# A transformer layer on one core: experts three deep, the routing weight applied as a root ahead of the square, all attention products on VectorE

## What is computed

```python
h = take(tok_weight, x)                                  # (8, 1024, 256)
h = h + attn(layernorm(h))                               # 16 heads of 16; softmax over the 8 positions
z = layernorm(h)
scores = sigmoid(z @ Wg.T)                               # 16 experts in 4 groups
# the best 2 groups, then the best 4 experts; w = 2.5 * score / sum of the four scores
out = sum_e w_e * (relu(z @ W1_e)**2 @ W2_e.T)           # cw[t, e] is 0 for an expert not chosen
h = h + out + relu(z @ Ws1.T)**2 @ Ws2.T                 # the shared expert, two slices wide here
```

## Time and profile before

| | |
|---|---|
| median of 3 runs | 1469.57 us (1466.58 to 1469.63) |
| the profiled execution | 1464.6 us |
| TensorE, matmuls busy | 1267.7 us, 87% |
| VectorE busy | 1189.9 us, 81% |
| ScalarE busy | 679.8 us, 46% |
| GpSimd busy | 689.5 us, 47% |
| mean granted TensorE clock | 0.961 |

### The profile page before, as it was taken

How to read it: one execution, slowest core, us unless ns; L and a number is a source line. 1 busy time by engine, 2 the same in 40 slices (tenths; PEclk the granted TensorE clock), 3 DMA queues, 4 the chain that set the end, 5 groups by cost and what they waited for, 6 DMA issues and landing times.

```text
span 1464.6 us, 22940 instructions
## 1 busy us (share of the span) xinstructions
PE 1267.7 (87%) x7488; PEld 1033.1 (71%) x7488; DVE 1189.9 (81%) x1792; ACT 679.8 (46%) x1138; POOL 689.5 (47%) x753
## 2 busy tenths in 40 slices
PE   4458898889888899888989889898988989989898
PEld 2146767768677687767778677776867768677787
DVE  3868889697987969789797888969798797978854
ACT  2234444544444454444544444454553445445355
POOL 7744535365263635535464363536526363442600
PEclk9579999999999999999999999999999999999999
DMA  2302111111211112111111212112121111212122
GB/s 66 125 16 74 58 60 58 61 62 55 73 62 57 58 44 88 58 61 58 66 65 44 78 67 62 58 46 73 58 73 58 61 58 44 88 44 73 59 73 73
DMA packets 33748, 92.21 MB, mean 63 GB/s; under 512 B 4800, under 2 KB 13376, under 8 KB 33600
## 3 DMA queue, kind: packets, MB, share of 16 engines
q1 hardware_dynamic: 30528, 81.99, 16.7%
q0 software_dynamic: 3072, 8.39, 2.0%
HBM read 81.46 MB, written 8.91 MB: 62 GB/s over the span
## 4 chain that ended last, share of the span: by engine, by line
DVE 39%; PE 31%; issue 19%; POOL 5%; ACT 5%; DMA 1%; DVEq 1%; ACTq 0%; POOLq 0%; SPq 0%
PE psY L900 9%; PE psH L887 8%; DVE ring L684 7%; PE psB L927 5%; DVE p_sb L641 5%; DVE hid_lo L647 5%; PE psA L966 3%; DVE g_gt L723 2%; DVE ring L300 2%; PE psA L978 2%; DVE ring L302 2%; DVE ring L279 1%; DVE k_sb L666 1%; ACT hid_hi L510 1%; DVE stats L659 1%
## 5 line engine op out<-in xcount | busy, mean ns | idle before, releaser
L900 PE MATMUL psY<-w_hi,hid_hi 128*128 128x256 f32 x1152 | 339.0, 294 | 53.6 <-DVE hid_lo L647 50.3
L510 ACT CAST hid_hi<-p_sb 128x512 fp32r<-128x512 f32 x256 | 159.2, 622 | 388.8 <-DVE p_sb L641 379.5
L900 PE MATMUL psY<-w_lo,hid_hi 128*128 128x256 f32 x1152 | 330.5, 287 | 0.0
L900 PE MATMUL psY<-w_hi,hid_lo 128*128 128x256 f32 x1152 | 330.2, 287 | 0.0
L279 POOL TENSOR_TENSOR ring<-q_sb,k_sb 128x1024 f32<-128x1024 f32 x64 | 169.1, 2653 | 309.1 <-PE psA L940 205.2
L900 PEld LDWEIGHTS psY<-w_hi,hid_hi 128*128 128x128 f32 x1152 | 223.6, 194 | 107.4 <-DVE hid_lo L647 72.6
L647 DVE TENSOR_TENSOR hid_lo<-p_sb,hid_hi 128x512 fp32r<-128x512 f32 x256 | 214.6, 838 | 93.4 <-ACT hid_hi L510 73.7
L887 PE MATMUL psH<-xT_hi,w_hi 128*128 128x512 f32 x576 | 235.6, 409 | 10.9 <-issue 8.7
L641 DVE TENSOR_TENSOR p_sb<-r_sb,cwB 128x512 f32<-128x512 f32 x256 | 214.2, 837 | 34.1 <-ACT r_sb L499 27.2
L900 PEld LDWEIGHTS psY<-w_lo,hid_hi 128*128 128x128 f32 x1152 | 224.6, 195 | 9.8
L887 PE MATMUL psH<-xT_lo,w_hi 128*128 128x512 f32 x576 | 230.2, 400 | 0.0
(11 more groups left out here) (133 smaller groups left out, 2137.5 us busy)
## 6 DMA issues: line engine op xcount, KB each, us to landing
cwB<-cw_dram SPq DMA_DIRECT2D x128, 512.0 KB, 3.7
out<-h SPq DMA_DIRECT2D x32, 256.0 KB, 5.4
p_sb<-w_t SPq DMA_DIRECT2D x3, 512.0 KB
cwB<-w_t SPq DMA_DIRECT2D x3, 512.0 KB, 4.5
h<-w_t SPq DMA_DIRECT2D x2, 512.0 KB
xin<-table,idx_now POOLq DMA_INDIRECT x56
cwB<-wqkv_t SPq DMA_DIRECT2D x2, 384.0 KB, 3.2
cw_dram<-cwT SPq DMA_DIRECT2D x16, 32.0 KB, 1.6
```

Source lines behind the costliest of these rows:

```text
L510: nc.scalar.copy(hid[0][:, e % 2, :], src[:, e % 2, :]).then_inc(hid_hi, 1)
L900: last = nc.tensor.matmul(psY[:, j // 2, (j % 2) * D:(j % 2 + 1) * D], hid[a][:, e % 2, j * P:(j + 1) * P], W2[b][:, e, :], start=(e == 0 ...
```

## The change

The block loops are written out in full (`nth` is now plain arithmetic, the registers and `idx_now` are gone). A block's head and attention have one list of 72 places in place of two lists of 36, so head b+2 now reaches as far as the first weighted values, and the attention of b+1 the rest. `hid` gets a third buffer and `up` is issued three experts ahead. VectorE takes relu and weight in one instruction straight from `psH`, with the root of the weight; ScalarE squares twice, once to `p_sb` in float32 and once rounded to `hid`. The root is made on GpSimd in two `pow`: of the 64 sigmoid denominators a partition, and of the 4 sums. All eight products are on VectorE; the scaling of both norms is on ScalarE (with a new tile `nmr` of minus mean times root, from GpSimd); the sums go to a tile `o_sb`, their split to `xT2`; the scores stand in `psB`. The weights arrive in 14 pieces over eight staging buffers, and the first experts wait only for their own pieces.

```diff
+    R = 3
+    AHEAD = 3
...
-        hid = [sb(f"hid_{p}", [P, 2, T], f32r) for p in ("hi", "lo")]
+        hid = [sb(f"hid_{p}", [P, R, T], f32r) for p in ("hi", "lo")]
...
+        T1 = 9
+        QKV_AT = [13, 13, 14, 15, 16, 17]
+        SCORES = [20, 23, 27, 29]
+        SPREADS = [34, 34, 36, 37, 39, 39, 41, 42]
+        OUT_PROJECTION, T2, LOGITS, WEIGHTS = 49, 53, 54, 65
...
+        V_PRODUCTS = [14, 16, 18, 19, 22, 22, 25, 27]
+        V_MAX, V_SUM, V_PROBS, V_OUT = 30, 30, 35, (46, 47)
+        V_VALUES = [35, 35, 38, 38, 41, 41, 43, 44]
...
+        V_ROUTE = [56, 57, 58, 61, 63, 63]
+        P_RSTD1, P_BIAS, P_RSTD2, P_GATHER, P_ROOT, P_ROOTSUM = 4, 27, 50, 52, 56, 65
...
+            def root_of_scores(blk):
+                pool.wait_ge(route_step, nth(blk, ROUTE_STEPS, ROUTE_FIRST[1] + 1))
+                nc.gpsimd.tensor_tensor(lgt[:, :, :], sig[:, :, :], half_neg[:, :].unsqueeze(2).to_broadcast([P, TT, E]),
+                                        ALU.pow).then_inc(root_ready, 1)
+
+            def root_of_sum(blk):
+                pool.wait_ge(route_step, nth(blk, ROUTE_STEPS, ROUTE_FIRST[5] + 4))
+                nc.gpsimd.tensor_tensor(w_rec[:, :], w_sum[:, :], half_neg[:, :], ALU.pow).then_inc(root_ready, 1)
...
+            def square(n):
+                b, e = n // X_ALL, n % X_ALL
                 if e < SH:
...
+                up_taken(act, n)
...
+                wait(act, hid_lo, n - 1)
+                nc.scalar.activation(p_sb[:, n % 2, :], r_sb[:, n % 2, :], ACT.Square)
+                wait(act, w2_mm, n - R + 1)
+                nc.scalar.activation(hid[0][:, n % R, :], r_sb[:, n % 2, :], ACT.Square).then_inc(hid_hi, 1)
...
+            def weigh(n):
...
+                dve.wait_ge(h_mm, n + 1)
+                wait(dve, hid_hi, n - 1)
...
+                nc.vector.scalar_tensor_tensor(r_sb[:, n % 2, :], psH[:, n % 2, :], 0.0, cwB[:, (r // QN) % 2, r % QN, :],
+                                               ALU.max, ALU.mult).then_inc(weighed, 1)
...
+            def step_of(blk, e):
+                n = blk * X_ALL + e
+                if n + 2 < B * X_ALL:
+                    weigh(n + 2)
+                if n + 1 < B * X_ALL:
+                    hidden_lo(n + 1)
+                if e == 0 and blk > 0:
+                    add_experts(blk - 1)
...
+                for h in (2 * e, 2 * e + 1):
+                    stage_of(blk + 1, HALF + h)
+                    stage_of(blk + 2, h)
```

More of the change, by code:

```diff
@@ L122, in lm_tower_layer @@
         rstd = [sb(f"rstd{w}", [P, TT]) for w in range(2)]
+        nmr = [sb(f"nmr{w}", [P, TT]) for w in range(2)]
         lg = sb("lg", [P, TT, 2, E])
@@ L160, in lm_tower_layer @@
         small_in = sem("small_in")
-        w_in = [sem(f"w_in{k}") for k in range(STAGES)]
+        w_in = [sem(f"w_in{k}") for k in range(14)]
         w_hi = sem("w_hi")
@@ new lines, in normalise @@
+            def normalise(w, blk, src, dst):
+                act.wait_ge(ln_rstd[w], nth(blk, 1, 1))
+                if w == 0:
+                    wait(act, prod_ready[1], nth(blk, LP, 0))
+                d = dst[:, :, :].rearrange("p a t -> p (a t)").rearrange("p (j d) -> p j d", d=D)
+                for j in range(TT):
+                    last = nc.scalar.activation(d[:, j, :], src[:, j, :], ACT.Identity,
+                                                bias=nmr[w][:, j:j + 1], scale=rstd[w][:, j:j + 1])
+                last.then_inc(xn_ready[w], 1)
@@ L613, in _ @@
[L613 to L617 removed]
+            for p in range(HALF):
+                stage_of(0, p)
+                if p == A_T1 + 2:
+                    act.wait_ge(const_step, CONST_ALL)
+                    nc.scalar.copy(spread[:, :, :].rearrange("p a b -> p (a b)"),
+                                   rows(r_sb[:, :, :])).then_inc(spread_ready, 1)
@@ L620, in _ @@
+            for h in range(HALF):
+                stage_of(0, HALF + h)
+                for k in range(PIECES_ATT, PIECES_ALL):
+                    if HI_AT[k - PIECES_ATT] == h:
+                        weight_hi(k)
+                if h == SQ_0:
+                    square(0)
+                    square(1)
+                stage_of(1, h)
+            for b in range(B):
+                for e in range(X_ALL):
+                    step_of(b, e)
         @block.vector
         def _(dve):
-            dve.sem_inc(hid_lo, CREDIT)
```

672 lines of the change are left out of this document (317 added, 355 removed).

## The result

| | before | changed |
|---|---|---|
| median | 1469.6 us (4 runs) | 1351.34 us (4 runs, 1350.70 to 1351.89) |
| ratio | | 0.920, 95% interval 0.918 to 0.922 |
| profiled execution | 1464.6 us | 1350.1 us |
| mean granted TensorE clock | 0.961 | 0.975 |

The account below looks back on a forecast made before the run. Bound: TensorE and VectorE handing over, 13.5 us of TensorE waits in each 87.1 us block. Forecast: 199.5 + 13 x 81.5 + 65 + 49.5 + 5.6 = 1379, plus 5.0 to the median: 1384 us, range 1345 to 1460.

Parts of the forecast that it names:

- The chain S, projection, next S: One block followed from the end of its scores (S) to its projection and on to the next S: 81.5 us.
- S to P: From the end of a block's scores to the start of its projection, VectorE's work and waits: 38.6 us.
- P to S: From a block's projection to the end of the next scores, TensorE's work: 40.4 us, with VectorE covering it.
- my first rival: In the blocks, VectorE stays the bound and each missed wait counts in full: 1417 to 1460 us, chance 0.17.
- one stretch of the half clock in a block, as now, about 1.7: In each block TensorE runs once at half clock, as before the change: about 1.7 us added.
- my second rival: In the blocks, TensorE runs through and the clock stays up: 77.5 to 79 a block, 1335 to 1350 us, chance 0.08.
- The start: To the first expert addition: q, k, v 6 us later; products 3, routing 4.5, splits 3 earlier; 199.5 us in all.
- The loops: At the loop's seven turns, TensorE's and VectorE's idle time goes when written out: 7 to 13 us in all.
- The roots: GpSimd's pow on 64 numbers takes 5 to 8 us, hidden; up to about 11 it costs nothing.
- Rival 3: The big pow holds VectorE's second input, delaying routing, products and hid_lo: 1525 us, chance 0.09.
- rival 4: The pow is slow but holds nothing; cw comes 4 to 6 us late: 1430 us, chance 0.06.
- Rivals 1 and 5: VectorE stays the bound (1435 us, 0.17); or straight code stalls or waits move whole to the spreading (1460 to 1475, 0.05).

Follow-up runs that it names:

- u4: The changed kernel with the scaling of both norms on VectorE again in place of ScalarE: 1402.7 us.
- b1_straight: The kernel before with only its block loops written out on all five engines: 1442.9 us, ratio 0.983.
- r1: The changed kernel with GpSimd's pow on 64 numbers made a multiplication and the products of odd number back on GpSimd: 1384.6 us.
- n2: The changed kernel with q, k, v not waiting for all constants, and third expert's up and first down ahead of block 1's first spreading: 1344.7 us.
- n3: The changed kernel with the start of n2, and VectorE adding a block's experts ahead of the next weight and low part: 1349.4 us.
- r0: The changed kernel with GpSimd's pow on 64 numbers replaced by a multiplication, so the routing weights are not the reference's: 1344.8 us.
- u5: The changed kernel with two experts in flight and the order of a step that belongs to two: 1561.2 us.
- p2: The changed kernel with GpSimd's pow on 64 numbers issued twice in a row: 1487.1 us.
- u2: The changed kernel with two experts in flight, keeping the step order made for three: 1724.1 us.
- u3: The changed kernel with the expert as before (relu, square, weight from SBUF, rounding; no root), three in flight: 1710.0 us.

## Why the prediction was right, and where it was not

**The chain S, projection, next S: right as a method, and its parts.** The block is set by VectorE from S to P and by TensorE from P to S, as I had it; u4 shows both. VectorE is busy for 34.3 of the 36.6 us from S to P (its waits are 0.7 for the exponential, 0.8 for the spreading and 0.4 for ScalarE's roundings), and TensorE in all of P to S. S to P: 38.6 forecast, 36.6 measured. The mis-sized terms: I let VectorE wait 2.8 us for ScalarE in the softmax and it waited 0.7 (8.1 us from S to the end of the split for 9.5), and the 1.5 for ScalarE held by the fourth sum was nothing; the 0.8 for the spreading I did not have. Eight values are 9.1 for 9.7 and the splits 1.6 for 2.1, against which my 1.5 for overlap stands. Six expert steps with their contention were 10.0 for 10.3, the two sums 4.4 as forecast. P to S: 40.4 forecast, 41.7 measured.

One sum of mine was wrong: 49.6, 8.3, 2.8, 3.7, 4.2 and 4 make 72.6 us of TensorE a block and not 73.6, so its waits were 14.5 and not 13.5. The forecast of the block does not use it, only my first rival does. In the changed kernel TensorE is busy for 75.3 of the 78.2 us.

**The clock: the term that failed in the blocks.** I kept "one stretch of the half clock in a block, as now, about 1.7", and gave 0.8 for what is left. None came. By the numbers: 81.5 - 2.0 + 1.3 - 1.7 - 0.8 = 78.3. For the blocks this is my second rival, "the clock stays up", 77.5 to 79 a block, at 0.08.

But the 1.7 did not belong in the sum in the first place. I added it to a chain whose part from S to P is VectorE's, and that is the part in which the half clock mostly lay before. The kernel before has two blocks that are alike but for this, the first without a half clock and the third with 3.4 us of it. By stretch, and what TensorE waited for `hid_lo` in each:

```profile
200.60:286.86 86.26, 76.29 (x467) 62.29 (x465) 74.31 (x112) 40.80 (x69) 41.92 (x46) 1.00 0.19 63
375.64:461.94 86.30, 77.85 (x467) 63.68 (x465) 74.36 (x112) 40.90 (x69) 41.93 (x46) 0.98 0.19 62
```

```profile
PE psY L900 <- DVE hid_lo L647: 5.1, 3, 3.2
PE psY L900 <- DVE hid_lo L647: 3.6, 3, 1.7
```

They are equally long. What TensorE lost to the clock it waited less for VectorE. In u4, too, S to P grew by no more than VectorE's work, with 3.4 us of half clock in it. Where TensorE is the one that is waited for, the half clock does cost: in b1_straight 3.4 us of it leave S to P at 36.5 us in twelve blocks, and in the block in which 3.2 of it fall into P to S, that stretch takes 50.1 us for 48.7; in r1 it takes 45.4 for 43.3 in the one block with 3.4 us of it. In the block before the last, which is mostly TensorE's, 3.4, 6.8 and 13.7 us of it go with 64.6 (n2), 66.5 (changed) and 70.5 us (n3).

What brings it on these runs show only in part. In the blocks of the changed kernel, of n2, of n3 and of r0 up to the block before the last, where TensorE waits 1.5 us at most at a time, there is none; in u4, with one wait of 2.9 more, 3.4 us of each block are at it; in u5, with waits of 2.2 to 2.5 in several places, 12.2. But the first block of the kernel before has waits of 3.2 and 2.5 us and no half clock, and one block of r1 has 3.4 us of it with no wait over 1.5.

**The start: wrong by 15 us.** 200.6 was before, 199.5 within 8 was forecast, 214.3 came. My differences for block 0's attention (6 - 3 - 4.5 - 3) come to 4.5 us earlier, and block 1's scores did end 4.4 earlier, at 123.71 us for 128.16, though not by the terms that I gave: that the routing would gain 4.5 was wrong, since the first `cw` reached TensorE at 120.6 us for 112.0. The term that failed is "but more of block 1 is done before", for which 3.4 us were left in the sum. The two stretches from the end of block 1's scores to the first addition, before and changed:

```profile
128.16:200.60 72.44, 64.99 (x385) 56.20 (x386) 61.06 (x99) 35.70 (x62) 36.76 (x44) 0.98 0.14 49
```

```profile
123.71:214.32 90.61, 81.48 (x487) 67.86 (x486) 76.41 (x119) 38.38 (x67) 45.82 (x48) 0.94 0.19 65
```

It is 18.2 us more, with 102 matmuls more in it. In TensorE's list block 0's experts stand, in the new 72 places, further behind block 1's attention: the first `down` comes behind block 1's scores and first spreading, and waits 7.2 us for that softmax, where before it stood ahead of both. The first addition now falls 12.9 us behind the end of block 2's scores, and fell 13.2 ahead of it. The order showed this, and I did not follow it there. Moving the first `down` alone ahead of the spreading does not undo it (at most 0.8 us in n2).

**The loops: right sign, half the size.** 7 to 13 us, measured 23.6. I priced the idle time that stood at the turns; what makes up the rest stays open (the register arithmetic, or stalls handed on). Of my bound for the fetching of straight code, 0 to 13, nothing shows: the "issue" waits of TensorE before `up` (8.7 us in 5) and of VectorE before the products (9.3 in 6) are gone in b1_straight.

**Relu and weight from PSUM, products, scalings: right in size, partly in price.** 0.68, 1.23 and 0.59 us stand where 0.69, 1.21 and 0.4 to 0.69 were forecast, VectorE's sum is 68.5 us a block for 70.4. `hid_lo` stayed at 0.82 (six of eight sums run beside it). The Trainium skill ("ScalarE: Activation LUTs", Rules for kernel authors) would leave additions and multiplications to VectorE; the estimate from its figures was 0.59 us, and the trace agrees with it (0.591). The rule's advice cost 51 us here (u4), since VectorE is the one that S to P waits for.

**The roots: outside my 5 to 8, inside the bounds.** 10.55 us, above the middle between 1.04 and 16.7. "Up to about 11 it costs nothing" was nearly so: 0.6 us a block, through the bias addition that it pushes onto the routing. Rival 3 is refuted by r0 and p2, rival 4 had the right mechanism (`cw` late by what is over the slack) with p2's numbers, 8.4 a block. By the Trainium skill ("GPSIMD Engine Reference", Key points) GpSimd shares its SBUF interface with VectorE; the trace agrees for additions (`e_eq` 2.42 us under the bias) and multiplications (r1), and shows no trace of it for `pow`, of either width.

**Waits of TensorE.** Forecast 3 us before the first spreading and 2 before the projection; measured 1.0 and 0.4, and 1.5 for the experts' addition, which I had not listed. Rivals 1 and 5 are out: VectorE is the bound in one stretch only, and no wait moved whole.

What stays open is how the gain divides. The loops with their registers are 24 us of 118. For the rest, each of four parts taken away made a kernel slower (the third buffer, the root, the scaling on ScalarE, and the products on VectorE, these in r0), and the third buffer given alone to the kernel before did too; the new order of 72 places was never run by itself.

## What to carry to other kernels

Cut a pipelined block where two engines must meet, and write down for each stretch whose instructions have no gap: work moved off that engine counts in full there and nothing in the other stretch. A deeper pipeline, a shorter hand-over, an earlier input and the order inside a step belong together; one of them alone can be slower than none. Charge a loss of one engine, its half clock too, only in a stretch where the others wait for it. For a change of the order, follow each engine's list through the first block too, and count what now stands ahead of the first result, since the start is paid once, but in full.

## What the runs showed of the hardware

- The half clock costs where TensorE is waited for, and hid behind VectorE elsewhere: 3.4 us of it in a block of the kernel before made no difference (86.30 us for 86.26), and in b1_straight none from S to P, but 1.4 us when 3.2 of it fell into P to S (50.1 for 48.7). At the half clock a 512 wide matmul starts 0.43 us after the one before, for 0.23.
- The granted clock was 1.00 all through the blocks of the changed kernel, where TensorE's longest wait was 1.5 us; it fell to 0.5 for 3.4 us of a block with one wait of 2.9 us more (u4), and for 12.2 (u5) and 15.4 us (u2, u3) with many. It did not fall in the first block of the kernel before, with waits of 3.2 and 2.5 us.
- A `pow` on GpSimd takes 1.04 us for 4 numbers a partition and 10.55 for 64, 0.16 us for each further one, and stretched none of VectorE's instructions with two SBUF inputs that ran inside it (p2); a multiplication of the 64 takes 0.29 (r0).
- Seven turns of a loop on five engines, with the register arithmetic that goes with them, cost 23.6 us, 3.4 a turn, where the longest idle time at a turn was 1.9 us.
